# A ring of six row tiles between the two layer norms, with a smaller x staging buffer and three steps moved to other beats

## The reference

```python
u = x @ in_proj_w.T + in_proj_b                  # 512 -> 1536
uc = conv1d(u, short_w, 3 taps, causal) + short_b
x0, x1, v = split(uc, 3)
k = filter_k(...)                                # small sine network times a decay, once for all sequences
v = fftconv(v * x1, k, filter_bias)              # causal long convolution over the 512 positions
x = layernorm(x + (v * x0) @ out_proj_w.T + out_proj_b)
gate = silu(qlinear(x, wq_gate, s_gate))         # 512 -> 1408, integer codes and one scale per row
up = qlinear(x, wq_up, s_up)
x = layernorm(x + qlinear(gate * up, wq_down, s_down))
```

## Time and profile before

| | |
|---|---|
| median of three runs | 1161.1 us |
| profiled execution, its own time | 1163.3 us |
| its span in the profile | 1161.5 us |
| mean granted TensorE clock | 0.966 of full speed |
| PE busy | 1071.9 us, 92% of the span |
| DVE, POOL, ACT busy | 727.5, 630.0, 467.5 us |
| two halves in the steady part (an even and an odd one) | 131 us |

### The profile page before, as it was taken

One profiled execution on the slowest core, in us unless ns is written; L12 is line 12 of the kernel. 1 busy time (PEld: TensorE's weight loads), 2 busy tenths in 40 slices (PEclk: granted clock), 3 DMA queues, 4 the chain that ended last, 5 costly groups with the idle time before them and its releaser, 6 DMA issues.

```text
span 1161.5 us, 18427 instructions
## 1 busy us (share of the span) xinstructions
PE 1071.9 (92%) x6634; PEld 873.1 (75%) x6634; DVE 727.5 (63%) x1327; ACT 467.5 (40%) x995; POOL 630.0 (54%) x677
## 2 busy tenths in 40 slices
PE   5896869999999999999999999999999999979996
PEld 3565658787877787787877787787877788867774
DVE  5665546576666767576666767576666667564443
ACT  3365434433434344433434344343434344322332
POOL 0147565566564666566564666566574667575211
PEclk9797879999999999999999999999999999989998
DMA  5155321222122212222122212222122221212332
GB/s 159 60 172 166 124 99 42 67 66 74 55 74 82 74 55 64 76 68 76 54 74 83 73 56 64 65 73 73 55 74 55 73 56 41 87 46 91 100 91 82
DMA packets 52216, 90.60 MB, mean 78 GB/s; under 512 B 6362, under 2 KB 11098, under 8 KB 52126
## 3 DMA queue, kind: packets, MB, share of 16 engines
q1 hardware_dynamic: 49072, 85.25, 24.3%
q10 hardware_dynamic: 3054, 4.18, 1.1%
HBM read 78.14 MB, written 11.27 MB: 77 GB/s over the span
## 4 chain that ended last, share of the span: by engine, by line
PE 70%; DVE 12%; ACT 7%; issue 6%; POOL 4%; DMA 1%; ACTq 0%; POOLq 0%; SPq 0%; DVEq 0%
PE bank L744 11%; PE bank L746 10%; PE bank L745 10%; PE gate_up L871 10%; PE gate_up L872 10%; PE down L882 6%; PE down L883 5%; ACT cx L473 3%; DVE hid_lo L734 2%; DVE cx L643 2%; DVE tmp L670 2%; ACT x L505 1%; PE bank L856 1%; PE spectrum L744 1%; PE spectrum L745 1%
## 5 line engine op out<-in xcount | busy, mean ns | idle before, releaser
L551 POOL TENSOR_TENSOR acc<-acc,tmp 128x256 f32<-128x256 f32 x160 | 126.1, 788 | 162.4 <-DVE tmp L670 156.0
L670 DVE TENSOR_TENSOR tmp<-spectrum,filt 128x512 f32<-128x512 f32 x256 | 173.4, 681 | 0.0
L744 PE MATMUL bank<-xT_hi,win_hi 128*128 128x512 f32 x384 | 163.1, 425 | 6.8 <-DVE cv L646 4.1
L871 PE MATMUL gate_up<-x2T_hi,wg_sb 128*128 128x256 f16 x704 | 167.4, 278 | 0.0
L872 PE MATMUL gate_up<-x2T_lo,wg_sb 128*128 128x256 f16 x704 | 165.5, 275 | 0.0
L871 PE MATMUL gate_up<-x2T_hi,wu_sb 128*128 128x256 f16 x704 | 164.2, 274 | 0.0
L872 PE MATMUL gate_up<-x2T_lo,wu_sb 128*128 128x256 f16 x704 | 164.0, 273 | 0.0
L728 DVE SCALAR_TENSOR_TENSOR hid<-gate_up,up_scale,hid 128x256 f32<-128x256 f32 x176 | 84.9, 482 | 125.4 <-ACT hid L521 125.4
L745 PE MATMUL bank<-xT_lo,win_hi 128*128 128x512 f32 x384 | 156.3, 407 | 0.0
L746 PE MATMUL bank<-xT_hi,win_lo 128*128 128x512 f32 x384 | 156.0, 406 | 0.0
L882 PE MATMUL down<-wd_sb,hid_hi 128*128 128x512 f32 x352 | 148.8, 423 | 6.1 <-DVE tmp L693 4.6
(11 more groups left out here) (110 smaller groups left out, 2276.8 us busy)
## 6 DMA issues: line engine op xcount, KB each, us to landing
wd_sb<-wd_scratch SPq DMA_DIRECT2D x176, 256.0 KB, 2.6
xstage<-in_x SPq DMA_DIRECT2D x32, 256.0 KB, 4.4
x<-in_x SPq DMA_DIRECT2D x32, 256.0 KB, 2.7
out<-x SPq DMA_DIRECT2D x32, 256.0 KB, 3.2
x<-in_win SPq DMA_DIRECT2D x12, 256.0 KB, 2.9
x2T_lo<-in_wd SPq DMA_DIRECT2D x6, 256.0 KB, 2.8
wd_scratch<-x2T_lo ACTq DMA_DIRECT2D x6, 256.0 KB, 2.0
x<-in_wd SPq DMA_DIRECT2D x5, 256.0 KB, 2.8
```

Source lines behind the costliest of these rows:

```text
L551: G.tensor_tensor(acc[:, i, 0, :], acc[:, i, 0, :], t[:, 1, :], ALU.subtract)
L670: TT(dst, spectrum[j % 2][:, :, :], k_part, ALU.mult).then_inc(made_done, 1)
L744: mm(out_ap, ah, bh, start=k == 0, stop=False)
L871: mm(dst, w[:, kb, rows(q)], x2T_hi[:, kb, ts], start=kb == 0, stop=False)
```

## The change

Tile `x2` gets six slots, used as a ring: tile b of half m is in slot `(2m+b) % 6`. The load of half m then waits for the store of half m-3, which is issued a half before. `xstage` keeps two tiles. Tiles 0 and 1 of a sequence are loaded in beat 10, two halves ahead, as before; tiles 2 and 3 are loaded into the same two places in beat 9 of the half that transposes them, after the transposes of tiles 0 and 1. Four steps move: LN2's `norm` from beat 5 to beat 6 (its stores to beat 7), `resid` from beat 5 to beat 3, both `xsplit` pairs from the head of the next beat to the end of beats 9 and 10, and the code loads from one block ahead of the list into the list, each four codes ahead of its conversion. The code slots in `x2` move to slots 4 and 5; the first sequence's tiles 2 and 3 are staged there too.

```diff
     earlier = shared(n, beat - 1) if beat else shared(n - 1, HB - 1)
-    steps += readers([p for p in earlier if p[0] != "x2t"]) + shared(n, beat)
+    steps += readers([p for p in earlier if p[0] not in ("xt", "x2t")]) + shared(n, beat)
...
     if beat == 4 and done:
         steps += [("stat", LN2, n - 4, 0), ("stat", LN2, n - 4, 1), ("var", LN2, n - 4)]
-    if beat == 5 and done:
+    if beat == 6 and done:
         steps += [("norm", LN2, n - 4)]
+    if beat == 7 and done:
         steps += [("store", n - 4, 0), ("store", n - 4, 1)]
-    if beat == 5 and out:
+    if beat == 3 and out:
         steps += [("resid", n - 2, 0), ("resid", n - 2, 1)]
...
     if beat == 9 and out:
         steps += [("norm", LN1, n - 2)]
+    if beat in (9, 10):
+        steps += readers([p for p in shared(n, beat) if p[0] == "xt"])
     for i, ready in enumerate((1, 4, 7, 9)):
         if beat == ready and convs:
             steps += [("psplit", n - 1, i)]
+    if beat == 9 and n % 2 == 1 and n + 1 < HALVES:
+        steps += [("xload", (n + 1) // 2, tb) for tb in (2, 3)]
     if beat == 10 and n % 2 == 1 and n + 3 < HALVES:
-        steps += [("xload", (n + 3) // 2, tb) for tb in range(TB)]
+        steps += [("xload", (n + 3) // 2, tb) for tb in (0, 1)]
...
-        xstage = sb("xstage", [P, TB, D], F32)
+        xstage = sb("xstage", [P, 2, D], F32)
...
-        x2 = sb("x2", [P, TB, D], F32)
+        x2 = sb("x2", [P, SLOTS, D], F32)
...
-        code_slots = [flat(x2T_lo[:, 0:2, :].bitcast(F32)), flat(x2T_lo[:, 2:4, :].bitcast(F32)), x2[:, 2, :], x2[:, 3, :]]
+        code_slots = [flat(x2T_lo[:, 0:2, :].bitcast(F32)), flat(x2T_lo[:, 2:4, :].bitcast(F32)), x2[:, 4, :], x2[:, 5, :]]
...
+        def x_tile(s, tb):
+            return x2[:, 2 + tb, :] if s == 0 and tb >= 2 else xstage[:, tb % 2, :]
+
+        def slot_of(m, b):
+
+            return (2 * m + b) % SLOTS, (2 * m + b) // SLOTS
...
             def load_x(s, tb):
-                if s:
-                    sp.wait_ge(bank_ready, use["xt", s - 1, tb] + 1)
+                if s and tb >= 2:
+                    sp.wait_ge(bank_ready, use["xt", s, tb - 2] + 1)
+                elif s > 1:
+                    sp.wait_ge(bank_ready, use["xt", s - 1, tb + 2] + 1)
+                elif s:
+                    sp.wait_ge(bank_ready, use["xt", 0, tb] + 1)
                 row = (s * TB + tb) * P
-                sp.dma_start(xstage[:, tb, :], x[row:row + P, :]).then_inc(x_in[tb], 16)
+                sp.dma_start(x_tile(s, tb), x[row:row + P, :]).then_inc(x_in[tb], 16)
...
-                if k < 4 and n >= 2:
-                    sp.wait_ge(stage_used, NFLOAT)
+                if n >= 2 and k < 4:
+                    sp.wait_ge(bank_ready, use["xt", 0, n] + 1)
                 elif k >= 4 and codes[k - 4][2] is None:
...
-            for tb in range(TB):
+            for tb in range(2):
                 load_x(1, tb)
             sp.wait_ge(k_mm, TB)
             sp.dma_start(down_scale[:, :], down_row).then_inc(late_in, 16)
             sp.dma_start(out_bias[:, :], out_row).then_inc(late_in, 16)
-            for k in range(NCODE):
+            for k in range(4):
                 load_code(k)
 
             for kind, *at in steps:
                 if kind == "xload":
                     load_x(*at)
+                elif kind == "code" and at[0] + 4 < NCODE:
+                    load_code(at[0] + 4)
                 elif kind == "wdload":
                     m, q = at
                     index = HB * m + q
...
                 elif kind == "store":
                     m, b = at
-                    tb = pair_block(m, b)
+                    slot, _ = slot_of(m, b)
                     sp.wait_ge(ln_done[LN2], 2 * m + b + 1)
-                    row = (m // 2 * TB + tb) * P
-                    sp.dma_start(out[row:row + P, :], x2[:, tb, :]).then_inc(stored[tb], 16)
+                    row = (2 * m + b) * P
+                    sp.dma_start(out[row:row + P, :], x2[:, slot, :]).then_inc(stored[slot], 16)
                 elif kind == "resid":
                     m, b = at
-                    tb = pair_block(m, b)
-                    if m >= 2:
-                        sp.wait_ge(stored[tb], 16 * (m // 2))
-                    elif m == 1:
+                    slot, past = slot_of(m, b)
+                    if past:
+                        sp.wait_ge(stored[slot], 16 * past)
+                    elif m == 2:
                         sp.wait_ge(code_done, NCODE)
                         sp.wait_ge(wd_saved[2], 16 * saves_before[2][NCODE])
                         sp.wait_ge(wd_saved[3], 16 * saves_before[3][NCODE])
-                    row = (m // 2 * TB + tb) * P
-                    sp.dma_start(x2[:, tb, :], x[row:row + P, :]).then_inc(res_in[tb], 16)
-            for tb in range(TB):
-                sp.wait_ge(stored[tb], 16 * NSEQ)
+                    row = (2 * m + b) * P
+                    sp.dma_start(x2[:, slot, :], x[row:row + P, :]).then_inc(res_in[slot], 16)
...
-                    tb = pair_block(m, b)
-                    pool.wait_ge(res_in[tb], 16 * (m // 2 + 1))
+                    slot, past = slot_of(m, b)
+                    pool.wait_ge(res_in[slot], 16 * (past + 1))
```

More of the change, by code:

```diff
@@ L32 @@
 ACT = mybir.ActivationFunctionType
-NFLOAT, NGATE, NCODE = 18, 24, 35
+NFLOAT, NCODE = 18, 35
+SLOTS = 6
 def unit(n, beat):
@@ L243, in build @@
         x_in = [sem(f"x_in{n}") for n in range(TB)]
-        res_in = [sem(f"res_in{n}") for n in range(TB)]
-        stored = [sem(f"stored{n}") for n in range(TB)]
+        res_in = [sem(f"res_in{n}") for n in range(SLOTS)]
+        stored = [sem(f"stored{n}") for n in range(SLOTS)]
         stage_hi, stage_used, code_done = sem("stage_hi"), sem("stage_used"), sem("code_done")
@@ L409, in _ @@
                         sp.wait_ge(wd_saved[3], 16 * saves_before[3][NCODE])
-                    row = (m // 2 * TB + tb) * P
-                    sp.dma_start(x2[:, tb, :], x[row:row + P, :]).then_inc(res_in[tb], 16)
-            for tb in range(TB):
-                sp.wait_ge(stored[tb], 16 * NSEQ)
+                    row = (2 * m + b) * P
+                    sp.dma_start(x2[:, slot, :], x[row:row + P, :]).then_inc(res_in[slot], 16)
+            for slot in range(SLOTS):
+                sp.wait_ge(stored[slot], 16 * len(range(slot, 2 * HALVES, SLOTS)))
         @block.scalar
@@ L503, in _ @@
                     for b in range(2):
-                        tb = pair_block(m, b)
-                        A(x2[:, tb, :], x2[:, tb, :], ACT.Identity, scale=rstd[:, w, b:b + 1],
+                        slot, _ = slot_of(m, b)
+                        A(x2[:, slot, :], x2[:, slot, :], ACT.Identity, scale=rstd[:, w, b:b + 1],
                           bias=shift[:, w, b:b + 1]).then_inc(ln_done[w], 1)
@@ L565, in _ @@
                     m, b = at
[L566 to L567 removed]
+                    slot, past = slot_of(m, b)
+                    pool.wait_ge(res_in[slot], 16 * (past + 1))
                     if m == 0:
                         pool.wait_ge(late_in, 32)
[L570 removed]
+                    G.tensor_tensor(x2[:, slot, :], x2[:, slot, :], out_bias[:, :], ALU.add).then_inc(res_biased, 1)
                 elif kind == "x2add":
                     m, b = at
[L573 removed]
+                    slot, _ = slot_of(m, b)
                     pool.wait_ge(made_done, made["ln2", m, b] + 1)
[L575 removed]
+                    G.tensor_tensor(x2[:, slot, :], x2[:, slot, :], flat(temp_of(("ln2", m, b))), ALU.add).then_inc(temp_added, 1)
                 elif kind == "var":
@@ L681, in _ @@
                     k = use["op", m, b]
-                    tb = pair_block(m, b)
+                    slot, _ = slot_of(m, b)
                     dve.wait_ge(bank_ready, k + 1)
                     dve.wait_ge(res_biased, 2 * m + b + 1)
-                    TT(x2[:, tb, :], bank[k % 2][:, :], x2[:, tb, :], ALU.add).then_inc(bank_read, 1)
+                    TT(x2[:, slot, :], bank[k % 2][:, :], x2[:, slot, :], ALU.add).then_inc(bank_read, 1)
                 elif kind == "ln2":
@@ L699, in _ @@
                         dve.wait_ge(temp_added, temp["ln2", m, b] + 1)
-                    Vv.bn_stats(stats[:, w, b, :], x2[:, pair_block(m, b), :]).then_inc(ln_stat[w], 1)
+                    Vv.bn_stats(stats[:, w, b, :], x2[:, slot_of(m, b)[0], :]).then_inc(ln_stat[w], 1)
                 elif kind == "var":
@@ L799, in _ @@
                     for c in range(CB):
-                        last = nc.tensor.transpose(dst[:, rows(c)], xstage[:, tb, rows(c)], ident[:, :])
+                        last = nc.tensor.transpose(dst[:, rows(c)], x_tile(s, tb)[:, rows(c)], ident[:, :])
                     last.then_inc(bank_ready, 1)
@@ L855, in _ @@
                     for c in range(CB):
-                        last = nc.tensor.transpose(dst[:, rows(c)], x2[:, pair_block(m, b), rows(c)], ident[:, :])
```

(1 more changed line is left out.)

4 lines of the change are left out of this document (removed).

## The result

The changed kernel is slower: 1170.2 us as the median of five runs (1169.7 to 1173.6), against 1161.9 us (1160.5 to 1164.2) for the kernel before in the same comparison, a ratio of 1.0064 with a 95% interval of 1.004 to 1.0088. The forecast was 1157.6 us, with 1148 to 1167 as its range. The profiled run took 1173.6 us with a span of 1171.8 (before: 1163.3 and 1161.5). It is the slowest of the five: its mean granted clock is 0.957, that of the median run 0.963, and that of the kernel before 0.966.

What follows compares the result with a forecast made beforehand. PE, busy 92% of the span, was taken as the bound, so only its waits or clock cost time. Terms -14.2 + 10.8 + 0.3 + 2.4 - 4.2 + 1.4 = -3.5 us gave 1157.6 us for the median, range 1148 to 1167.

Steps and rivals of the forecast that it cites:

- LN2's norm to beat 6: First op of beat 6, halves 4 to 15: twelve PE waits of 1.18 us go, gaining 14.2 us.
- Residual loads and additions in beat 3: POOL's additions delay acc_lo, so iv starts 0.9 us late in twelve halves: 10.8 us lost, and 0.3 in half 3.
- the far bound, 4.4 us: Upper bound for the residual landing, the median of a group of four loads; it makes iv 2.2 us late.
- rival C: Slow clock stays behind all six waits in beat 10 add 8.5 us: 1166.1 us; chance 0.08.
- Rivals B: Residual rows land late, at 3.8 us, delaying iv in thirteen halves: 5.6 us slower, 1166.7 us; chance 0.18.
- xt (+2.4): Second xt pair in beat 10: tiles 2 and 3, fetched between the pairs, come 0.4 us late six times, 2.4 us lost.
- Filling (-4.2): Halves 1 and 2: 5.0 us gained before x2t of half 3, 0.8 lost to late x tiles; 4.2 us gained.
- Draining (+1.4): Half 16: additions push acc_lo by 3.4 us, all seen; waits of 0.83 and 1.11 us go; net 1.4 us lost.
- the signs of the quiet halves: Signs for right: iv waits about 0.9 us, POOL waits 1.5 to 2 us per half, x2t of half 3 near 161 us.
- the sign for wrong: A residual landing under 2.8 or over 3.5 us, or PE's 1.18 us wait still there.
- The sign for an even and an odd half together: Sign for right in the steady part: two halves together take 131 us less about 0.1.

Runs made afterwards that it cites:

- the ring version: Changed kernel with x tiles 2 and 3 loaded in beat 8 into free ring slots, additions still in beat 3: 1159.7 us, ratio 0.9957.
- the best version: Changed kernel with the bias additions back in beat 5 and x tiles 2 and 3 loaded in beat 8 into free ring slots: 1127.3 us, ratio 0.9697.
- the late split: The best version with the xT split back at the head of the next beat, behind acc_hi on ACT: 1138.9 us, ratio 0.9774.

## Why the prediction was wrong

- **LN2's norm to beat 6 (-14.2).** Right where it stands alone. The waits went, ACT's idle time hid the norm in beat 6, and with `iv` in time the move is worth 17 us: 14.2 of idle time and 12 x 0.27 of PE's busy time, a size that the prediction did not have. Within the changed kernel it is worth 2, not clear of the noise, since the new wait stood ahead of it and took its place. The prediction said that the new wait eats most of the gain; it ate all.
- **Residual loads and additions in beat 3 (+11.1).** This is the step that failed. Place and mechanism were right, and seven halves came out at 0.9 us. Wrong was the assumption that one landing time, 3.1 us, holds in all halves. In five of twelve halves a landing took 3.6 to 4.9 us and `iv` was 1.5 to 2.2 us late. The second tile may indeed come 0.9 us after the first unseen (in the quiet halves it came 0.6 to 1.3 after it and POOL did not wait), but in halves 5 and 11 it came 2.0 and 2.5 after it. The waits sum to 16.1 us instead of 11.1. The longer ones also brought the clock down, which the shorter ones did not: with them gone (additions in beat 5) or with the landing out of the way (loads in beat 1), the kernel is 29 us faster. The row with the far bound, 4.4 us, was in hand and was used for the range alone: a price that can only rise with the tail of the landings was set by their lower middle. The rule of the Trainium skill, "DMA: Bandwidth & Descriptors" (Anatomy of one DMA), is fitted to DMAs that GpSimd issues; carried over to SP's it gives an estimate of 2.6 us for these 256 KB. The down weights, issued by SP, do take 2.6 (176 of them, median), and the residual rows of the kernel before took 2.7 (median). The residual rows of the changed kernel, issued within 1 us behind a load of down weights, took 2.9 to 4.9, so for them the measurement decides against it.
- **The clock (rival C, 0.08).** This is the second step that failed: the sum puts the clock at nothing. It was tied to the six waits at `xt` only; the new waits at `iv` were not counted as causes, though the long ones are of the same size. It added 12.5 us of busy time in the profiled run, more than the longer waits, and somewhat less in the median run with its clock of 0.963. Without these 12.5 us the profiled run would have come to about 1161 us (an estimate), where 1159.8 was forecast for it. Rivals B (late rows) and C came together, and the range had room for one of them only.
- **xt (+2.4).** Right in size for the waits (+2.2). But the wait for xT_lo would have been 1.27 us without the late tiles, as the ring version shows, and the clock fell behind three of six, not one. In ring slots the x tiles are worth 12 us.
- **Filling (-4.2).** The total came out, -4.0, but by luck. At 77 us the changed kernel was 1.1 ahead. From there to 122 us, in half 1, it lost 3.5, not 0.8, and not by late x tiles (`xt` waited 1.97 us, 2.01 before): two stays at the lower clock, at 77.81 and 91.46, are new in this trace and come to 3.4. From there to `x2t` of half 3 it gained 6.4, not 5.0; PE's waits over 1 us fell from 11.8 to 8.7, and the rest is fewer slow stretches.
- **Draining (+1.4).** The wait at `iv` of half 16 grew by 4.3 us (3.04 to 7.32), 3.4 forecast. Still the half became 2.1 us shorter. The waits of 0.83 and 1.11 went as forecast. Most of the rest is clock again, this time a gain that I had not costed, and luck: in this half the slow stretches sum to 6.9 us before (1020 to 1050) and to 3.4 after (1050 to 1065), and a third of the latter falls into the wait at `iv` itself.
- **What would show it.** All the signs of the quiet halves came (POOL's wait of 1.7 us, a quiet half 63.2 us long instead of 63.5, `x2t` of half 3 at 161.97), and so did the sign for wrong: a residual landing over 3.5 us. The sign for an even and an odd half together, 0.1 us less, did not come: over the thirteen steady halves two of them took 2.6 us more.

## What to carry over

A transfer whose consumer stands ahead of critical work on an in-order engine must be priced by its slowest landing, not by its middle; put the load where it has room for that, or the consumer behind the critical work. Either gave about 29 us here. Where the busiest engine's waits can bring its clock down, a wait of 1.8 us may cost twice its length, so cutting six waits from 1.8 to 1.3 us was worth some 9 us in the median (3 to 15 by the interval), where 3.2 were expected. When a buffer is widened (the ring), look for the stretch in which its new slots are empty: here they could stand in for the staging that the same change had taken away.

## What the runs showed of the hardware

- In the steady parts of these kernels no wait of PE of up to 1.3 us (twelve of 1.18 us before, six of 1.27 in the best version) was followed by a stretch at the lower of its two levels. Of waits of 1.5 to 2.3 us many were, though not always the same ones: one of six before, seven of eleven after, two of six with the additions in beat 5, five of six with the late split. A stay costs 1.6 us and more. In the best version, whose steady part has no such wait, the four runs lie within 1.3 us; with the late split they lie within 11.
- A wait of PE costs more than its idle time: 0.27 us of added busy time for a wait of 1.18 us (62.31 against 62.04 us for half 8, and much the same in six more halves of the same two kernels).
- The residual rows, two loads of 256 KB issued within 1 us behind a load of down weights on SP's queue, took 2.9 to 4.9 us to land (median 3.3); as a pair by themselves, in the kernel before, they took 2.7 (median). The late ones stood in the same five halves whichever rows or slots they used, and in other halves when they were issued two beats earlier.
- SP's issue of one such load took 1.3 us in half 8 of the changed kernel, with a median of 0.4 over all 32.
